# Two layers of a graph network: who scales the second half of the last normalization

## The reference, cut to what matters

```python
x = _layernorm(x + _L0_gnn_ref(x, edge_attr_3, ..., edge_index), axis=-1)
x = _layernorm(x + _L1_gnn_ref(x, edge_attr_64, src, dst, ...), axis=-1)

def _layernorm(x, axis=-1, eps=1e-05):
    m = jnp.mean(x, axis=axis, keepdims=True)
    v = jnp.var(x, axis=axis, keepdims=True)
    return (x - m) / jnp.sqrt(v + eps)
```

## Time and profile before

| what | value |
|---|---|
| median of three runs | 751.61 us |
| the profiled execution | 751.49 us |
| its span, first to last instruction | 749.5 us |
| busy: PE, DVE, ACT, POOL | 584.5, 447.9, 378.0, 380.3 us |
| last instruction of VectorE ends | 746.35 us |
| last store issued | 747.56 us |

### The profile page before, as it was taken

The page is one execution under the profiler, slowest core; times in us unless marked ns, Lnnn a source line. Parts: engine busy times, 40 slices in busy tenths (PEclk is TensorE's granted clock), DMA queues, the critical chain, the costliest instruction groups (busy, mean ns, idle before and its releaser), DMA issues.

```text
span 749.5 us, 16666 instructions
## 1 busy us (share of the span) xinstructions
PE 584.5 (78%) x4159; PEld 437.7 (58%) x4160; DVE 447.9 (60%) x1622; ACT 378.0 (50%) x663; POOL 380.3 (51%) x382
## 2 busy tenths in 40 slices
PE   4448787778877698797778877888877699879994
PEld 2336566666666566575666656766656577634433
DVE  7946566445655555555656555556554657588955
ACT  8245655565646555566555554656622224362044
POOL 6766566465655556655655555656667661000000
PEclk9967998689899869979979987998989667789997
DMA  6422233333424233332424323242322150000002
GB/s 128 109 59 72 59 96 76 73 77 75 95 58 95 55 91 77 77 89 57 98 57 95 85 64 82 68 96 63 89 41 50 40 97 7 2 0 1 1 1 43
DMA packets 89135, 48.70 MB, mean 65 GB/s; under 512 B 76253, under 2 KB 77668, under 8 KB 89070
## 3 DMA queue, kind: packets, MB, share of 16 engines
q1 hardware_dynamic: 75949, 35.40, 19.3%
q0 software_dynamic: 11968, 12.28, 8.3%
q10 hardware_dynamic: 1152, 0.16, 0.1%
HBM read 46.86 MB, written 0.93 MB: 64 GB/s over the span
## 4 chain that ended last, share of the span: by engine, by line
PE 61%; issue 15%; DVE 9%; another core or an unknown queue 7%; ACT 4%; ACTq 1%; DMA 0%; SPq 0%; DVEq 0%
PE ps L638 15%; PE ps L601 15%; PE ps L678 14%; PE ps L623 6%; DVE pair L1686 3%; PE ps L617 2%; PE ps L607 2%; ACT adj L1007 1%; PE ps L871 1%; PE ps L591 1%; PE ps L628 1%; PE ps L824 1%; PE ps L899 1%; PE ps L587 1%
## 5 line engine op out<-in xcount | busy, mean ns | idle before, releaser
L528 POOL DMA_INDIRECT rows<-in_x,idx x374 | 379.0, 1013 | 241.8 <-issue 93.9
L601 PE MATMUL ps<-pair,ohp 128*125 128x500 bf16 x416 | 188.8, 456 | 35.9 <-ACT adj L1007 15.2
L1007 ACT CAST adj<-ps 125x500 f32 x208 | 123.8, 595 | 163.9 <-remote 84.9
L678 PE MATMUL ps<-whot,rows 128*128 128x108 f32 x816 | 194.9, 326 | 9.1 <-issue 8.4
L638 PE MATMUL ps<-xs,u 125*128 125x192 bf16 x1050 | 157.1, 276 | 56.1 <-issue 50.5
L678 PEld LDWEIGHTS ps<-whot,rows 128*128 128x128 f32 x816 | 159.5, 232 | 28.9 <-issue 22.3
L1303 DVE TENSOR_SCALAR pair<-iota_h,comb 128x500 bf16<-128x500 int16 x416 | 123.2, 358 | 71.9 <-remote 33.7
L994 ACT ACTIVATE u<-u,own 128x768 uint8<-128x768 uint8 (+1 forms) x168 | 152.8, 962 | 20.9 <-DMA u<-codes_scratch 20.1
L638 PEld LDWEIGHTS ps<-xs,u 125*128 125x128 fp8e4 x1050 | 103.9, 112 | 96.4 <-issue 79.8
L1318 DVE TENSOR_TENSOR agg<-agg,ps 128x24 f32 x416 | 76.0, 183 | 128.1 <-remote 63.7
L1307 DVE TENSOR_SCALAR ohp<-iota_h,srcp 128x125 bf16<-128x125 int16 x416 | 111.1, 278 | 10.2 <-issue 8.1
(11 more groups left out here) (211 smaller groups left out, 383.4 us busy)
## 6 DMA issues: line engine op xcount, KB each, us to landing
u<-codes_scratch SPq DMA_DIRECT2D x42, 400.0 KB
rows<-in_edge_attr SPq DMA_DIRECT2D x51, 256.0 KB
rows<-in_x,idx POOLq DMA_INDIRECT x374
x_now<-in_x SPq DMA_DIRECT2D x25, 31.2 KB
adj<-in_x SPq DMA_DIRECT2D x1, 700.0 KB
xs<-in_x SPq DMA_DIRECT2D x1, 700.0 KB
out<-u SPq DMA_DIRECT2D x3, 224.0 KB
adj<-in_edge_attr SPq DMA_DIRECT2D x1, 576.0 KB
```

The costliest lines, as they stand in the source:

```text
L528: pool.indirect_dma_start(rows[:, s, t, 0:C], None, x, bass.IndirectOffsetOnAxis(ap=idx[:, at:at + 1], axis=0)).then_inc(gathered[0][0] if ...
L601: return nc.tensor.matmul(m_ps[0:PN, bank_of(phase, g), 0:PAIRS], ohp[:, par, t, :], pair[:, par, t, :], start=(n == 0), stop=(n == GROUP ...
L678: last = nc.tensor.matmul(z_ps[:, half, at:at + ZW], rows[:, s, t, :], whot[:, par, t, :], start=True, stop=True)
L1007: nc.scalar.copy(bass.AP(adj, offset=start, ap=[[NT * NA, PN], [NA, NT], [1, GWIN]]), m_ps[0:PN, bank_of(phase, g), 0:PAIRS].rearrange("p ...
```

## The change

The four copies of each group leave ScalarE. GpSimd does them as one product of 125 x 256, with the same expression as VectorE's, after the waits for its two flags. SP waits for the semaphore `out_pool_ready` in place of `out_act_ready`.

```diff
@@ SP @@
                 sp.wait_ge(out_ready, b + 1)
                 if len(bank_tiles(1, b)) > TPA:
-                    sp.wait_ge(out_act_ready, b + 1)
+                    sp.wait_ge(out_pool_ready, b + 1)
@@ GpSimd, at the end of its program @@
             with pool.If(flag1 > 0):
                 pool.wait_ge(x1_stored, 16)
                 gather_again(x1_dram, 1)
+
+            for b in range(NB):
+                ts = bank_tiles(1, b)[TPA:]
+                if len(ts) > 0:
+                    pool.wait_ge(ln_rstd_ready[1], b + 1)
+                    pool.wait_ge(ln_centred[1], b + 1)
+                    nc.gpsimd.tensor_tensor(
+                        res[:, ts[0]:ts[-1] + 1, :], h[:, ts[0]:ts[-1] + 1, :],
+                        ln_rstd[:, ts[0]:ts[-1] + 1].rearrange("p (t a) -> p t a", a=1).to_broadcast([PN, len(ts), C]),
+                        ALU.mult).then_inc(out_pool_ready, 1)
@@ ScalarE, the last loop @@
                 if k < NB:
                     square(1, k)
-                if k >= 1 and len(bank_tiles(1, k - 1)) > TPA:
-                    act.wait_ge(ln_rstd_ready[1], k)
-                    for j in bank_tiles(1, k - 1)[TPA:]:
-                        last = nc.scalar.activation(res[:, j, :], h[:, j, :], ACT.Copy, scale=ln_rstd[:, j:j + 1])
-                    last.then_inc(out_act_ready, 1)
```

More of the change, by code:

```diff
@@ L320, in gnn_two_layers @@
         scaled_dve, scaled_act, y_turned = sem("scaled_dve"), sem("scaled_act"), sem("y_turned")
-        x1_centred, out_act_ready = sem("x1_centred"), sem("out_act_ready")
+        x1_centred, out_pool_ready = sem("x1_centred"), sem("out_pool_ready")
         u_act_ready, u_dve_ready = sem("u_act_ready"), sem("u_dve_ready")
```

## The result

The changed kernel took 751.73 us, the median of 22 runs, beside 748.86 us for the kernel before (also 22, the three known ahead among them). The recorded ratio, which leaves out the few executions in a slower state, is 1.0084, with a 95% interval of 1.0056 to 1.0113: 6.3 us slower, 4.2 to 8.5. The two lists of times don't give that much by themselves. Their medians lie 2.87 us apart, which is 0.38%, and their means 2.6 us. The whole times thus show that the kernel got slower, and by how much only roughly. The median of before was 751.61 when only three runs were known; over 22 it is 2.75 us lower. The 4.4 us of the forecast on top of 748.86 would be 753.3.

A forecast was written before the change was run, and what follows sets the result against it. The chain is mostly TensorE, but the edit acts only in the last 9 us of the 749.5 us span. GpSimd's late drain makes the span 753.9: 751.49 + 4.4 = 755.9 us; range 750.9 to 757.3, own part 754.8 to 756.8.

The forecast's parts named there:

- The 4.4 us of the forecast: End of program: span grows to 753.9 us because GpSimd's drain follows its last product; added to 751.49 us.
- The drain: GpSimd's closing drain: clears work left by gathers, so it takes 8.32 us after the last product, ending at 753.66.
- the first rival: End of program: the late drain costs nothing and only the earlier stores count, 751.1 us; chance 0.17.
- The product: Each group's GpSimd product: takes 0.60 us, middle of 0.44 and 0.76; third ends between 745.13 and 745.55.
- The copies that left ScalarE: Last normalization: twelve copies, 3.17 us, go; group 2's root starts 0.11 us earlier, single tile's product ends near 745.86.
- The stores: SP's stores of group 2: start between 745.03 and 745.77, gaining 0.37 us as the middle of 0.74 and nothing.
- That VectorE waits for GpSimd: Each group's product: every VectorE round grows by 0.60 us, span 754.85, time 756.8 us; chance 0.09.
- That the first product carries the leftover work: GpSimd's first product: starts 8.32 us late, at 749.04, giving 757.2 us; chance 0.05.
- the fourth: GpSimd at the end: late product and late drain both, span 759.4, time 761.4 us; chance 0.03.

The follow-up runs named there:

- The memset: Kernel before plus a one-column memset on GpSimd that waits for the third group's reciprocal: ratio 1.0011 (0.9966 to 1.0057), tail 17.34 us.
- the early drain: Changed kernel plus one more GpSimd drain just ahead of its three products: ratio to the kernel before 1.0015 (0.9976 to 1.0054), tail 13.19 us.
- the second comparison: The same change run again against the kernel before, on the 605 us chip: ratio 1.0068 (1.0032 to 1.0104), tail 18.05 us.
- the second queue: Kernel with the early drain, the smaller store of the last two groups issued by ScalarE, not SP: ratio to before 0.9985 (0.9949 to 1.0021), tail 13.28 us.

## Why the prediction was right

**The drain.** The step held in all its parts: the drain keeps its length when moved (8.37 us after the last product, 8.32 forecast), it comes after the products, and the rest of the engines wait for it. The memset shows that the place of the drain is enough, and the early drain shows that nothing else is needed. The forecast added 4.4 us to the span (4.36 before rounding), and the tail grew by 4.56. On the clock of before the last product ends at 745.43 for the forecast 745.34, which is 0.09; from its end the drain lasts 8.37 for 8.32 us, which is 0.05; the last 0.06 lies between the drain and the end of the span and is no more than the rounding of these times.

**The size of the ratio.** 0.6% was forecast. The recorded ratio is 0.84% in the first comparison (0.56 to 1.13) and 0.68% in the second (0.32 to 1.04); the medians alone give 0.38% and 0.72%. The tail's 4.56 us are 0.61% of 748.86 and lie inside both intervals. That the 1.7 us between 4.56 and 6.3 are scatter is likely by the second comparison, but not shown. The time itself proves little: 751.73 us is nearer to the 751.1 of the first rival than to the 755.9 of the forecast, because the first three runs of before happened to be long ones. It lies outside the forecast's own 754.8 to 756.8, and inside the whole range only because that reaches down to 750.9 to take in this rival. So far the number is luck; the mechanism is shown by the tail.

**The product.** Its length of 0.60 us, the middle of 0.44 and 0.76, is what it takes alone (0.61). It was forecast to end 0.60 or 1.02 us after VectorE's product starts; it ends 0.89 us after that, in between. The Trainium skill (SBUF — State Buffer, Who interferes with whom) has the two exclude each other, and the second one wait. This trace agrees in the direction, with VectorE, which is first, unharmed; the product got 0.24 us longer. That is less than the whole 0.37 us that were left of VectorE's product. It would still be a full wait if the first 0.13 us of GpSimd's instruction did not read the memory, and the sum had put 0.124 us to such a fixed part. No run tells these two apart. The copies that left ScalarE acted as forecast: on the clock of before its root of group 2 starts at 743.97 (forecast 743.97) and VectorE's product at 744.54 (744.53).

**The stores.** SP's first store of group 2 was to start 0.37 us earlier and starts 0.26 earlier: 739.15 + 6.36 = 745.51 against 745.77. The two groups before start 0.57 and 0.59 us earlier. One thing was missed: the four last issues take 2.11 us in place of 1.79. Here are the last three of SP's stores in two windows, the first with the end of group 2's:

```profile
739.51 1.31 SPq L503 DMA_DIRECT2D out<-u  x2
...
740.86 0.40 SPq L503 DMA_DIRECT2D out<-u  x1
```

The larger store of the single tile takes 0.73 us to issue, where it took 0.36. SP nevertheless branches at 742.4, which on the clock of before is 748.8, 0.3 earlier than 749.1: the first store of group 2 began 0.26 sooner, and the end follows that one (see the second queue above). So the step of the sum that let the end follow the last issue had the wrong cause, and it cost nothing only because the drain comes later. The single tile's product ends 0.47 us earlier (745.88 against 746.35; 745.86 was forecast) and brings nothing, as said.

**The rivals.** That the late drain costs nothing is refuted by the 5.0 us that SP waits. The Trainium skill (VectorE: DVE Perf Modes, The DRAIN you can't avoid) gives about 12 ns for the drains of the program's frame. SP's 13 ns agree with that, and GpSimd's 9236 ns do not. That VectorE waits for GpSimd: its products last 0.42 us as before. That the first product carries the leftover work: it starts 0.05 us after VectorE's and takes 0.84 us. With it falls the fourth.

## What to carry to other kernels

Before giving the first late work to an engine that has long been done, look at what that engine does at the end of its program. A drain, or any closing instruction, that hides now comes after the new work. On GpSimd after gathers it cost 82 ns for each of the last gathers (some 100 by that price) and 8.3 us in all, and one explicit drain in its idle time took it off the end. And in a kernel whose executions scatter by 1%, compare a stretch that starts from a fixed instruction: the tail told 0.3 us apart, five rounds of whole times told 0.4% apart.

## What the runs showed of the hardware that was not expected

- GpSimd's drain at a quiet moment: 1446 ns after 16 gathers, 5289 after 63, 6031 after 343, 8324 after 374 (the same in five kernels), 177 with none since the last drain. From 16 to 63 gathers it grows by 82 ns a gather and from 343 to 374 by 74. In between some 270 gathers have left nothing to pay for, for a reason that the traces don't name.
- Two products of 125 x 256 in fp32 from the same tile, one on VectorE and one on GpSimd: 0.42 us on VectorE with or without company, 0.61 on GpSimd alone and 0.85 when it starts 0.05 us after VectorE's.
- Issuing the smaller stores from a second queue shortened SP's issuing, and the wait for landing grew from 1.2 to 2.4 us; the landing came 3.2 to 3.4 us after the start of the third group's first store in either kernel.
